# New order lists for a fused attention, expert and state-space layer

## The chip, the cores and the metric

The kernel runs on one core of a Trainium2 chip. The metric is the device time of one execution in microseconds (us), lower is better. Engines are named as in the profile: PE (TensorE), ACT (ScalarE), DVE (VectorE), POOL (GpSimd) and SP (SyncE, which here issues every transfer).

## The reference

For x of 16 batches x 512 tokens x 128 features, four residual blocks follow one another:

```
x = x + attn(layernorm(x))       # 16 heads of 8; elu(.)+1, rotary; (q_rot k_rot^T)/(q k^T), then v, then w_out
x = x + ffn(layernorm(x))        # 8 experts, top 2, plus one shared; 128 -> 512 -> 128, exact gelu
x = x + scan(layernorm(x))       # W_in, causal conv of 4, silu, 16 states of h = dA*h + dt*B*x, y = C*h, norm, gate, W_out
x = x + ffn(layernorm(x))        # the same expert block again
```

## The kernel before

One batch is a tile of 128 features x 512 tokens. The batches go through a software pipeline of passes, and in pass i several batches are at different blocks at once. A part is named by a letter:

- **P**: preparation of batch i+1 (`P.load` turns x in, `P.mean`, `P.var`, four `P.qk` projections, four `P.til`, two `P.rope`, then eight `P.cast` on ACT that alternate with eight `P.rest` on POOL: they split the rotated tiles into bf16 parts). `P.pk` 0 to 3 on SP write those parts to DRAM, six transfers each. `P.keep` on POOL copies x aside, after the attention of the batch before is closed. `P.ahead` 0 and 1 and `A.load` 0 and 1 on SP bring the repacked heads back, groups k = 0 to 3. `load_heads` for k = 0 waits until all 24 writes have landed.
- **A**: attention of batch i, 64 units in 16 steps. In a unit `A.den` (PE, L708) makes the denominator scores in one of two banks, `A.ln` (ACT) takes their logarithm, `A.num` (PE, L713) makes the numerator scores in the only bank NUM, and `A.mul` (DVE, L1110) multiplies. `A.ex` (ACT) is the exponential of a step of four units, `A.av` (PE, L735) the product with v of a step. `A.oT`, then `A.close` on PE (L741) and DVE (L1115), end it; `A.v` is the v projection.
- **F**: first expert block (batch i-1), **M** and **N**: the scan (batch i-1 begins it as M, its last nine states follow in the next pass as N), **E**: the end of the scan, **G** and **H**: second expert block (begun as G, ended one pass later as H). In F, G and H `up` and `down` are the products of 36 chunks (L772 to L774, L783), `gelu` is on ACT, `part` on DVE, `add` on POOL; `w` on SP loads an expert's weights from a DRAM copy, `gate` its gate row.
- **W** (pass 0 only): `W.split` on DVE makes the high and low halves of an expert's first weight, `W.store` on SP writes them to the DRAM copy. The first `F.w` waits for all nine.
- **T** on ACT: a load of a table set (L1023), `T.gelu`, `T.log` or `T.silu`.

No planner runs at build time. The order of each engine's queue is written out in six dictionaries: `HEAD` (before pass 0), `FIRST` (pass 0), `SECOND` (pass 1), `MAIN` (passes 2 to 15; pass 2 without H, pass 15 without P), `LAST` (pass 16) and `END` (pass 17). `numbered` expands an entry such as `A.ln*4` into the next four numbers of that part; `passes` runs the lists. Every engine works strictly through its own list, and each entry first waits on its semaphores, so an entry whose data is late holds up all that stands behind it:

```
            run(head, -1)
            run(numbered(FIRST[name], 0), 0)
            run(numbered(SECOND[name], 0), 1)
            main = numbered(MAIN[name], KEPT)
```

The waits that matter at the opening of a pass are these: the first `A.den` waits for heads k = 0, `F.mean` on PE waits for the DVE's `A.close` (`s_x1_done`), `P.cast` n waits for `P.rest` n-1, `W.split` n (from 3 on) for the landing of `W.store` n-3, and `P.ahead` 1 for the last `A.num` of the batch.

Of the kernel before, what the change touches and what calls it, by code (L numbers as in the profile page):

```python
# [1383 lines left out]
```

## Time and profile before

| | us |
|---|---|
| median of 3 runs (lowest to highest) | 3860.93 (3859.01 to 3870.79) |
| the profiled execution, its own time | 3871.34 |
| its span, first to last instruction | 3869.4 |
| PE busy | 3456.1 (89%) |
| ACT busy | 3236.8 (84%) |
| DVE busy | 2746.1 (71%) |
| POOL busy | 1277.1 (33%) |
| table loads on ACT | 554, 710.8 us |

Busy shares are means over passes that differ much: the passes at either end hold only some of the parts. PE busy includes modelled matmul ends. A stage is therefore read by its own window, its own waits and its own timeline.

### The profile page before, as it was taken

What the parts mean: (1) busy time and instruction counts of PE and PEld (TensorE: products, weight loads), DVE (VectorE), ACT (ScalarE), POOL (GpSimd) and SP (SyncE); (2) the same over time, 40 slices, a digit from 0 to 9 for tenths busy, and PEclk for the clock granted to TensorE, in tenths of its full rate; (3) what the DMA queues carried; (4) which work ended last, traced back from release to release, by engine and by line L of the source; (5) the groups of instructions that cost most, each with busy time, mean ns of one, the idle gap of its engine ahead of it and who ended that gap; (6) DMA issues with size and microseconds to landing.
All of it is one profiled execution on the core that took longest, in us unless ns stands there. A gap on an engine that the chain in (4) does not pass through costs nothing. (4 is left out here: it accounts for less than half of the span.)

```text
span 3869.4 us, 38405 instructions
## 1 busy us (share of the span) xinstructions
PE 3456.1 (89%) x11446; PEld 1442.6 (37%) x11446; DVE 2746.1 (71%) x3513; ACT 3236.8 (84%) x4060; POOL 1277.1 (33%) x758
## 2 busy tenths in 40 slices
...
GB/s 147 46 136 61 117 123 184 143 148 160 121 174 131 176 138 178 152 122 195 116 185 123 179 148 140 168 122 175 142 169 133 185 145 134 179 99 160 122 127 101
DMA packets 214848, 552.02 MB, mean 143 GB/s; under 512 B 25105, under 2 KB 96626, under 8 KB 214642
## 3 DMA queue, kind: packets, MB, share of 16 engines
...
## 5 line engine op out<-in xcount | busy, mean ns | idle before, releaser
L783 PE MATMUL bank<-hF,wst 128*128 128x512 f32 x2304 | 1171.9, 625 | 25.3 <-DVE tmp L1180 20.8
L1110 DVE TENSOR_TENSOR rPool<-bank,rPool 128x512 f32<-128x512 f32 x1024 | 703.1, 687 | 559.7 <-PE bank L713 514.1
L885 ACT ACTIVATE hF<-bank,cols 128x512 f32<-128x512 f32 x1152 | 770.9, 686 | 253.9 <-PE bank L774 245.5
L1330 POOL TENSOR_TENSOR yM<-yM,ws 128x1024 f32<-128x1024 f32 x240 | 595.1, 2479 | 1026.1 <-DVE ws L1229 1023.7
L1023 ACT ACT_TABLE_LOAD x554 | 710.8, 1283 | 9.7
L885 ACT ACTIVATE rPool<-bank 128x512 f32<-128x512 f32 x1024 | 571.2, 596 | 162.4 <-PE bank L708 156.9
L772 PE MATMUL bank<-xnH,wst 128*128 128x512 f32 x1152 | 599.5, 520 | 68.5 <-DMA wst<-wscr 36.4
L1222 DVE TENSOR_TENSOR_SCAN ws<-dAs,ws 128x1024 f32<-128x1024 f32 x256 | 635.5, 2487 | 6.9 <-ACT dAs L885 5.5
L1315 POOL TENSOR_TENSOR acc<-acc,tmp 128x512 f32<-128x512 f32 x240 | 353.1, 1471 | 835.7 <-DVE tmp L1180 827.3
L783 PEld LDWEIGHTS bank<-hF,wst 128*128 128x128 f32 x2304 | 412.7, 193 | 434.4 <-issue 347.7
L713 PE MATMUL bank<-qpk,kpk 48*128 48x512 bf16 x1024 | 420.3, 410 | 122.6 <-DVE rPool L1110 122.0
L885 ACT ACTIVATE rPool<-rPool 128x2048 f32<-128x2048 f32 x256 | 489.8, 1913 | 3.6
L774 PE MATMUL bank<-xnH,wst 128*128 128x512 f32 x1152 | 460.5, 400 | 0.0
L708 PE MATMUL bank<-qpk,kpk 48*128 48x512 bf16 x1024 | 383.6, 415 | 85.4 <-issue 49.6
L773 PE MATMUL bank<-xnL,wst 128*128 128x512 f32 x1152 | 459.7, 399 | 0.0
L1218 DVE TENSOR_TENSOR ws<-bc,dtx 128x1024 f32<-128x1024 f32 x256 | 376.0, 1478 | 19.9 <-DMA bc<-bcscr 19.7
L772 PEld LDWEIGHTS bank<-xnH,wst 128*128 128x128 f32 x1152 | 220.0, 191 | 343.6 <-issue 192.5
L735 PE MATMUL bank<-rPool,vpad 128*32 128x512 f32 x2048 | 325.5, 677 | 2.0
L1180 DVE SCALAR_TENSOR_TENSOR tmp<-bank,cols,cB 128x512 f32<-128x512 f32 x256 | 190.4, 744 | 173.9 <-PE bank L783 162.9
L885 ACT ACTIVATE dAs<-dte,Acol 128x1024 f32<-128x1024 f32 x256 | 294.3, 1150 | 21.3 <-DVE ws L1222 18.3
L1229 DVE TENSOR_TENSOR ws<-bc,ws 128x1024 f32<-128x1024 f32 x240 | 308.0, 1289 | 2.6
L713 PEld LDWEIGHTS bank<-qpk,kpk 48*128 48x128 bf16 x1024 | 95.7, 93 | 550.5 <-DVE rPool L1110 389.3
...
## 6 DMA issues: line engine op xcount, KB each, us to landing
...
kpk<-kscr SPq DMA_DIRECT2D x128, 192.0 KB, 6.0
qpk<-qscr SPq DMA_DIRECT2D x128, 192.0 KB, 6.5
...
```

The lines of the kernel that those rows point to most:

```text
L708: pe.matmul(ps[n % 2][:, :], lhs, rhs, start=True, stop=True).then_inc(s_den, 1)
L713: pe.matmul(ps[NUM][:, :], lhs, rhs, start=True, stop=True).then_inc(s_num, 1)
L772: pe.matmul(bank, low, xnH[:, :], start=True, stop=False)
L773: pe.matmul(bank, high, xnL[:, :], start=False, stop=False)
L774: pe.matmul(bank, high, xnH[:, :], start=False, stop=True).then_inc(s_up, 1)
L783: pe.matmul(ps[FFN][:, :], w2, hF[:, (NCH * f + q) % HSLOTS, :], start=(c == 0), stop=(c == FC - 1)).then_inc(s_dn, 1)
L885: return nc.scalar.activation(out_, in_, fn, **kw)
L1023: act.preload_act_table_set({"log": LOG_EXP, "gelu": GELU_SET, "silu": SILU_SET}[name])
L1110: v.tensor_tensor(rP[:, slot, c, :], ps[NUM][:, :], rP[:, slot, c, :], ALU.mult).then_inc(s_mul, 1)
L1218: v.tensor_tensor(w, bc[:, s % 2, 0:1, :].broadcast_to(both), dtx[:, :, :], ALU.mult).then_inc(s_dbx, 1)
L1222: v.tensor_tensor_scan(w.rearrange("p h t -> p (h t)"), dAs[:, s % 2, :, :].rearrange("p h t -> p (h t)"), w.rearrange("p h t -> p (h t)") ...
L1330: g.tensor_tensor(yM[:, :, :], yM[:, :, :], ws[:, s % 3, :, :], ALU.add).then_inc(s_ya, 1)
```

## The change

All order lists get a new text. Operations, buffers, semaphores and the functions stay as they are. For every engine and every pass the new list holds the same entries the same number of times, with two exceptions on ACT: `SECOND` has 22 table loads where it had 24, and in `LAST` one `T.gelu` has become a `T.log` (50 table loads as before). Only the order within a pass changes. The core of the diff:

```
@@ HEAD @@
     "ACT": """
-    P.load P.mean P.var P.qk*4 P.cast*8
+    P.load P.mean P.var P.qk*2 P.cast*2 P.qk P.cast*2 P.qk P.cast*4
...
     "POOL": """
-    P.keep P.rope P.rest*4 P.rope P.rest*4
+    P.rope P.rest*4 P.rope P.rest*3 P.keep P.rest
@@ FIRST @@
     "SP": """
-    P.in W.store*7 A.load*2 P.pk*4 P.ahead*2 W.store*2
+    P.in W.store*7 A.load*2 W.store P.pk*4 P.ahead*2 W.store
     "PE": """
...
-    A.num*2 A.den*2 A.num A.av A.num A.den*2 A.num A.den A.num*2 A.av A.num A.den*3 A.num A.den A.num*2 A.den A.av
-    A.num A.den A.num A.den A.num*2 A.av A.num*3 A.av A.close
+    A.num A.den*3 A.num A.av A.num A.den*2 A.num*2 A.av A.den*2 A.num*2 A.den*4 A.num*2 A.av A.num A.den*2 A.num*3
+    A.den A.av A.num A.den*2 A.num*2 A.den A.num*4 A.av A.den A.num A.den A.num A.av A.num A.den*2 A.num A.av
+    A.num*4 A.av A.close
     "ACT": """
...
-    A.ex P.qk A.ln*4 A.ex P.qk A.ln*4 A.ex P.cast A.ln*4 A.ex A.ln*4 A.ex A.ln*4 A.ex P.cast A.ln*4 A.ex P.cast
-    A.ln*4 A.ex A.ln*4 A.ex P.cast A.ln*4 A.ex A.ln*4 A.ex P.cast*3 A.oT P.cast
+    A.ex P.qk A.ln*4 A.ex A.ln*4 P.cast A.ex A.ln*4 A.ex A.ln P.qk A.ln*2 P.cast*2 A.ln A.ex A.ln*6 A.ex A.ln*2 A.ex
+    A.ln P.cast A.ln*3 P.cast A.ln*2 P.cast A.ln A.ex A.ln A.ex A.ln*4 P.cast*2 A.ex A.ln*4 A.ex A.oT
     "DVE": """
-    W.split*2 A.v W.split A.mul*3 P.mean A.mul W.split A.mul W.split A.mul*2 P.var A.mul W.split A.mul*4 W.split
-    A.mul*4 W.split A.mul*4 P.til A.mul P.til A.mul P.til A.mul*6 W.split A.mul*4 P.til A.mul*32 A.close
+    W.split*4 A.v W.split*2 A.mul*2 W.split A.mul W.split A.mul P.mean A.mul*3 P.var A.mul*6 P.til A.mul*4 P.til
+    A.mul*6 P.til A.mul*9 W.split A.mul P.til A.mul*31 A.close
     "POOL": """
-    P.rope*2 P.rest*7 P.keep P.rest
+    P.rope P.rest*2 P.rope P.rest*6 P.keep
@@ SECOND @@
     "SP": """
-    F.w P.in F.w*3 F.rows F.gate*2 F.w*2 F.gate*2 F.w*2 F.gate F.w F.gate*3 A.load M.rows M.bc*2 A.load P.pk M.bc*5
-    P.pk*3 P.ahead*2
+    P.in F.w*3 F.rows F.gate*2 F.w*3 F.gate*3 F.w*2 F.gate*2 F.w F.gate A.load M.rows M.bc*3 A.load P.pk M.bc*2 P.pk
+    M.bc P.pk M.bc P.pk P.ahead*2
     "PE": """
-    A.v A.den*2 F.mean A.den A.num A.den*2 F.var A.den*2 F.router F.up*2 A.num F.up*2 A.num F.up F.down*2 A.den
+    A.v A.den F.mean A.den*3 A.num F.var A.den F.router F.up*4 A.num F.up A.den*2 F.down*2 A.den A.num F.up A.den*2
...
-    A.av A.num A.den*4 A.num*6 A.av*2 A.close
+    A.den*2 A.num*2 A.av A.num A.den*2 A.num A.den*2 A.num*7 A.av A.num A.av A.num A.av A.close
     "ACT": """
...
-    A.ln*4 M.decay A.ex A.ln M.decay P.cast A.ln*3 A.ex A.ln*4 A.ex A.ln*4 P.cast A.ex A.oT P.cast*2
+    M.decay*2 P.cast A.ln*2 A.ex A.ln*2 A.ex A.ln*2 P.cast A.ln*2 A.ex M.decay A.oT
     "POOL": """
-    F.add*5 P.rope F.add*2 M.take P.rest*4 P.rope M.acc*3 M.keep M.acc P.rest*3 M.acc P.rest P.keep M.acc
+    F.add*4 P.rope P.rest F.add*3 M.take P.rest P.rope M.acc*2 P.rest*6 M.acc*2 M.keep P.keep M.acc*2
@@ MAIN @@
     "SP": """
...
-    F.gate*2 F.w F.gate F.w F.gate F.w F.gate P.pk G.w F.gate G.rows G.gate*2 G.w*2 M.rows G.w A.load P.pk M.bc*4
-    G.w G.gate M.bc G.w*2 P.pk G.gate M.bc*2 P.pk G.gate P.ahead G.gate G.w P.ahead
+    A.load F.w F.gate*3 F.w F.gate*2 F.w P.pk G.w*2 G.rows P.pk*2 G.gate*2 G.w M.rows M.bc A.load M.bc*2 G.w*2
+    M.bc*2 G.w G.gate*2 P.pk M.bc*2 G.w P.ahead*2 G.w G.gate*2
     "PE": """
-    A.v H.down*2 A.den*2 H.down A.den*2 H.down H.up*2 F.mean A.num A.den H.down*2 H.up*2 A.num H.up*4 F.var A.num
+    H.down*2 A.den H.down A.den H.down A.den*3 A.v A.num A.den H.down F.mean H.up H.down H.up A.den A.num A.den
...
     "DVE": """
-    A.v H.part F.mean A.mul N.dbx A.mul N.scan N.dbx N.hc A.mul*2 H.part N.scan F.var N.hc H.part F.router A.mul
+    H.part A.v A.mul F.mean A.mul N.dbx*2 N.scan N.hc H.part A.mul N.scan F.var N.hc A.mul H.part F.router A.mul
...
@@ LAST @@
     "ACT": """
...
-    T.log G.router T.gelu G.gelu*3 M.mean T.log M.var T.gelu G.gelu M.xp*3 T.silu M.silu M.xp M.silu T.gelu G.gelu
-    M.row G.gelu M.dt G.gelu*2 M.dt T.log M.sp M.decay*2 T.gelu G.gelu*2 T.log M.decay T.gelu G.gelu*3 T.log
+    T.log G.router T.gelu G.gelu*3 M.mean T.log M.var T.gelu G.gelu M.xp*3 T.silu M.silu M.xp M.silu M.row T.gelu
+    G.gelu M.dt G.gelu*2 M.dt G.gelu T.log M.sp M.decay*2 T.silu M.silu T.log M.decay T.gelu G.gelu*4 T.log
```

## Rows read from the trace of the kernel before

**Rows 1.** The page's groups: table loads (count, busy, mean ns, idle before).

```profile
L1023 ACT ACT_TABLE_LOAD x554 | 710.8, 1283 | 9.7
```

**Rows 2.** Stages (pass 0; 1; 2; 3-14; 15-17): length; PE, PEld, DVE, ACT, POOL; clock; DMA.

```profile
75.80:198.10 122.30, 96.60 (x282) 18.53 (x283) 56.00 (x85) 77.56 (x101) 15.89 (x13) 0.65 0.23 69
198.10:416.90 218.80, 165.91 (x505) 58.18 (x504) 105.24 (x142) 151.36 (x190) 38.76 (x29) 0.73 0.31 94
416.90:647.10 230.20, 199.08 (x649) 80.93 (x649) 161.91 (x209) 193.43 (x242) 73.90 (x44) 0.89 0.46 141
...
647.10:3299.30 2652.20, 2514.71 (x8569) 1055.59 (x8568) 2017.37 (x2581) 2407.47 (x3037) 929.16 (x564) 0.98 0.50 153
3299.30:3869.40 570.10, 461.10 (x1409) 221.24 (x1407) 388.42 (x433) 392.95 (x471) 201.24 (x88) 0.91 0.39 130
```

**Rows 3.** Who waited for whom, 196 to 240 us: total, times, longest.

```profile
DVE xnF L1128 <- PE bank L674: 15.2, 1, 15.2
...
PE bank L708 <- DMA kpk<-kscr: 12.9, 1, 12.9
```

**Rows 4.** Timeline of DVE at the end of pass 0: A.close.

```profile
198.35 0.75 DVE L1115 SCALAR_TENSOR_TENSOR xFin<-bank,cols,xA 128x512 f32<-128x512 f32 x1 [4.77 <-PE bank L741]
```

**Rows 5.** Timeline of POOL at the end of pass 0: start, duration.

```profile
199.29 0.61 POOL L1310 COPY xA<-xP 128x512 f32<-128x512 f32 x1 [6.15 <-DVE xFin L1115]
199.86 1.15 POOL L1305 TENSOR_TENSOR parts<-til,parts 128x512 bf16<-128x512 f32 x1
```

**Rows 6.** Timelines of SP's issues, then of PE, at the opening of pass 1.

```profile
206.51 0.31 SPq L584 DMA_DIRECT2D kpk<-kscr  x1
...
221.05 0.32 SPq L595 DMA_DIRECT2D wst<-wscr  x1
...
196.24 2.07 PE L741 MATMUL bank<-oT,wos 128*128 128x512 f32 x2 [0.69 <-ACT oT L885]
...
212.89 1.01 PE L708 MATMUL bank<-qpk,kpk 48*128 48x512 bf16 x2 [12.88 <-DMA kpk<-kscr]
...
225.51 0.79 PE L772 MATMUL bank<-xnH,wst 128*128 128x512 f32 x1 [1.73 <-DMA wst<-wscr]
```

**Rows 7.** Timelines of ACT, POOL, SP and PE at the opening of pass 2.

```profile
414.14 0.60 ACT L885 ACTIVATE oT<-bank 128x512 f32<-128x512 f32 x1 [8.19 <-PE bank L735]
...
416.58 0.63 ACT L885 ACTIVATE parts<-til 128x512 bf16<-128x512 f32 x1 [1.32 <-POOL til L1305]
...
433.89 1.09 ACT L885 ACTIVATE rPool<-bank 128x512 f32<-128x512 f32 x2 [14.09 <-PE bank L708]
...
418.75 2.14 POOL L1305 TENSOR_TENSOR parts<-til,parts 128x512 bf16<-128x512 f32 x1
...
426.40 0.32 SPq L584 DMA_DIRECT2D kpk<-kscr  x1
...
433.21 1.01 PE L708 MATMUL bank<-qpk,kpk 48*128 48x512 bf16 x2 [14.64 <-issue]
```

**Rows 8.** Timeline of PE in the second half of pass 0: A.num, A.num, A.av, A.num.

```profile
172.54 0.60 PE L713 MATMUL bank<-qpk,kpk 48*128 48x512 bf16 x1 [0.79 <-DVE rPool L1110]
...
173.92 0.60 PE L713 MATMUL bank<-qpk,kpk 48*128 48x512 bf16 x1 [0.79 <-DVE rPool L1110]
...
174.46 1.93 PE L735 MATMUL bank<-rPool,vpad 128*32 128x512 f32 x8
...
176.32 0.60 PE L713 MATMUL bank<-qpk,kpk 48*128 48x512 bf16 x1
```

**Rows 9.** Timelines of SP and PE where pass 10 opens.

```profile
2193.15 0.32 SPq L584 DMA_DIRECT2D kpk<-kscr  x1
...
2199.94 0.59 PE L708 MATMUL bank<-qpk,kpk 48*128 48x512 bf16 x2 [0.52 <-issue]
```

**Rows 10.** Busy time and clock around the opening of pass 2.

```profile
345.00:417.00 72.00, 45.19 (x125) 7.78 (x125) 53.17 (x51) 41.57 (x50) 14.86 (x9) 0.52 0.20 65
...
433.00:470.00 37.00, 28.53 (x67) 10.94 (x68) 27.36 (x47) 30.73 (x38) 6.71 (x3) 0.50 0.42 128
```

More of the change, by code:

```diff
@@ L121 @@
-    M.scan A.mul M.hc A.mul*4 M.hc A.mul*3 M.dbx A.mul*4 M.scan A.close M.hc
+    A.v F.mean F.var A.mul*2 F.router F.route A.mul*2 F.turn F.part P.mean A.mul*3 F.part A.mul*3 F.part P.var
+    A.mul*3 F.part*2 A.mul*3 P.til*2 F.part A.mul F.part*2 A.mul*2 F.part M.mean A.mul P.til A.mul M.var A.mul
+    M.conv A.mul M.conv*4 A.mul M.conv*2 A.mul M.conv A.mul*4 P.til A.mul*3 M.dt M.dbx A.mul M.dbx A.mul M.scan*2
+    M.hc*2 A.mul*3 M.dbx A.mul M.scan A.mul*2 M.hc A.mul*2 M.dbx A.mul*2 M.dbx A.mul*3 M.scan A.mul M.hc A.mul*2
@@ L148 @@
-    G.up*2 A.close
+    H.down*2 A.den H.down A.den H.down A.den*3 A.v A.num A.den H.down F.mean H.up H.down H.up A.den A.num A.den
+    H.up*6 H.down*2 A.num F.var H.up*2 H.down*4 F.up A.num A.den*2 F.router A.av A.num A.den H.down*3 A.num A.den
+    H.down F.up F.turn F.up*2 A.num H.close P.load A.den*2 A.num F.down*2 P.mean F.down*2 A.num A.den P.var A.den
+    A.num F.up A.den F.up A.num A.av A.num F.up*5 A.av P.qk F.up A.num F.down*4 A.num A.den*2 P.qk A.den A.num
+    F.down A.den F.down A.num P.qk A.num A.den*2 F.up A.num A.av A.den A.num F.up*3 F.down*2 A.num F.up*2 F.down
@@ L169 @@
-    A.mul M.scan M.hc A.mul*2 G.part M.dbx A.mul M.scan M.hc A.mul M.dbx A.mul G.part A.mul M.scan A.mul M.hc
-    A.mul*5 G.part A.mul*2 M.dbx*2 M.scan*2 M.hc*2 A.close
+    H.part A.v A.mul F.mean A.mul N.dbx*2 N.scan N.hc H.part A.mul N.scan F.var N.hc A.mul H.part F.router A.mul
+    F.route N.dbx H.part F.turn A.mul N.dbx A.mul N.scan*2 A.mul P.mean N.hc A.mul*2 N.hc A.mul*2 F.part N.dbx P.var
+    N.dbx N.scan*2 N.hc A.mul F.part A.mul N.hc A.mul*4 N.dbx*2 A.mul N.scan P.til*2 F.part A.mul N.hc A.mul*2
@@ L171 @@
+    N.scan A.mul F.part A.mul*2 N.dbx N.scan P.til N.hc*2 F.part A.mul*2 E.mean F.part P.til A.mul*3 E.var A.mul
+    E.gate F.part A.mul G.mean A.mul*2 F.part A.mul G.var G.router G.route F.part G.turn M.mean A.mul M.var M.conv*8
+    G.part A.mul*7 M.dt M.dbx A.mul M.dbx M.scan M.hc A.mul*2 G.part M.scan A.mul M.dbx A.mul M.hc M.scan M.hc
+    A.mul*2 G.part A.mul*2 M.dbx*2 A.mul M.scan M.hc A.mul*2 G.part A.mul M.scan A.mul*4 M.hc A.mul*2 G.part A.mul*2
+    M.dbx*2 M.scan*2 M.hc*2 A.close
 """,
@@ L172 @@
     "POOL": """
-    N.acc H.add N.acc H.add*3 N.acc*4 F.add P.rope N.acc*3 F.add*2 P.rope P.rest F.add P.rest*2 F.add P.rest F.add*2
-    M.take P.rest*2 M.keep G.add M.acc P.rest M.acc*2 P.rest M.acc G.add*3 P.keep M.acc*2
+    H.add N.acc*2 H.add*3 N.acc*2 F.add N.acc*2 P.rope F.add N.acc*3 F.add*2 P.rest*4 F.add P.rope F.add*2 M.take
+    P.rest*3 G.add M.acc P.rest M.acc G.add M.acc M.keep M.acc G.add*2 M.acc*2 P.keep
 """,
@@ L208 @@
-    M.scan M.dbx M.hc M.scan G.part M.dbx M.scan M.hc*2
+    F.mean H.part N.dbx*2 N.scan*2 N.hc H.part N.dbx N.hc H.part F.var N.scan N.dbx H.part F.router N.scan N.hc
+    F.route N.hc N.dbx F.turn F.part N.scan N.dbx N.hc N.scan F.part N.dbx N.scan N.hc F.part N.hc F.part N.dbx*2
+    N.scan*2 N.hc*2 F.part E.mean F.part E.var F.part E.gate G.mean G.var F.part G.router G.route F.part G.turn
+    M.mean M.var M.conv*8 G.part*2 M.dt M.dbx*2 M.scan*2 M.hc*2 M.dbx M.scan M.dbx M.hc M.scan M.dbx M.scan M.hc*2
```

147 lines of the change are left out of this document (66 added, 81 removed).

## The prediction

> **What bounds the kernel now.** I read the page first, then the busy time by stage, then, for the stages with most idle time, who waited for whom, and last the timelines at the openings of the passes. By stage [rows 2] the twelve full passes take 2652.2 us, 221.0 each, and ACT is busy 2407.5 us of them (91%). There ACT's queue sets the pace; what is left of its idle time is many short waits of 0.3 to 1.3 us for a product of PE, because PE is in turn held at `A.num` by DVE. Pass 0 is different: in its second half PE has no other work, and the single bank NUM makes every unit a round trip PE, DVE, PE. The products start 1.38 us apart, and 2.40 us where an `A.av` lies between them [rows 8]. Pass 1 takes 218.8 us with ACT busy for only 151.4, pass 2 takes 230.2 with 193.4, and passes 15 to 17 take 570.1 with 392.9 [rows 2]. The loose time is there.
>
> Two single waits stand out. At the opening of pass 1 PE sits 12.9 us at the first `A.den`, until the heads of batch 1 land [rows 3, 6]. `F.mean` stands behind it in PE's list, so DVE's `F.mean` waits 15.2 us too [rows 3]. At the opening of pass 2 PE sits 14.64 us at the same place and ACT 14.09 us [rows 7]. In a steady pass the same load costs 0.52 us [rows 9].
>
> Both go back along one chain: last `P.rest`, last `P.pk` (six issues and their landing), `P.ahead` 0, heads landed. In pass 0 the last `P.rest` starts at 199.86 us, straight after `P.keep`, which could not run before the attention was closed [rows 5]; it ends at 201.0, `P.ahead` goes out at 206.51, PE goes on at 212.89 [rows 6]. The chain is 11.9 us. In pass 1 the last `P.cast` stands behind `A.oT` in ACT's list, at 416.58; its `P.rest` ends at 420.9 and PE goes on at 433.21 [rows 7]: 12.3 us.
>
> **The change part by part.**
>
> *Opening of pass 1.* In the new `FIRST` the last two casts stand behind `A.ln` 59, two steps before the end, and `P.keep` behind the last `P.rest`. Of PE's list 12 `A.num` and three `A.av` come after the `A.den` of that unit and before the last product: 12 x 1.38 + 3 x 1.02 = 19.6 us, and some 3.5 us more to `A.close`, so about 23 us before `A.close`. The two casts (0.63 each) and rests (1.15 each) and their hand-overs take 4 to 5 us, the chain 11.9. Heads can land some 7 us before `A.close`, which stands at 196.24 now [rows 6]. The wait goes, with a margin. What is late next? `F.mean` then waits for `A.close` on DVE, 198.35 + 0.75 = 199.1 [rows 4]; PE starts it at 199.3 instead of right behind the `A.den` pair of 212.89, at 213.9: 14.6 us sooner. The second candidate is the first expert weight. It is issued at 221.05 [rows 6], after the last two stores have landed, and the first `F.up` follows at 225.51, 1.73 of which it waits for that weight [rows 6]; all else was ready at 223.8, 9.9 us behind `F.mean`. In the new list only store 8 stands behind `P.ahead` 1, which waits for the last `A.num`, 3.5 us before the 196.24 of `A.close`. Ahead 1, the store and its landing (half the bytes that took 11 us there) give about 203, and the weight lands 4.5 us after its issue, by 209; `F.up` would be wanted at 199.3 + 9.9 = 209.2. That is level, so I take 14 us and not 16.
>
> *Head and pass 0.* The new head puts two casts before the third `P.qk` and two before the fourth, so the second `P.rope` waits for its tile and no longer for POOL, and the first heads come about 1 us sooner. Against it, the new `FIRST` puts four `W.split` ahead of `A.v` and two more ahead of the first `A.mul`. From the fourth on a split waits for a store's landing, and DVE holds all behind it. `A.v` on PE is two entries earlier in exchange. I take the one as used up by the other, with 2 us either way. For the rest of pass 0 I sum the round trips of PE's two lists, each the larger of 1.38 us and the work between two products (0.43 us for a `den`, a little under the 0.54 from the product at 173.92 to the `av` at 174.46; 1.02 more where an `av` is [rows 8]): 124.7 us for the old order, 128.3 for the new, because the new one puts up to three `A.den` into gaps that hold an `A.av` already. At the upper clock the two sums are 87.6 and 88.2. Pass 0 has both clocks, 0.65 on average [rows 2]. I take +1.5 us, between +0.6 and +3.6.
>
> *Opening of pass 2.* The new `SECOND` has the last cast behind `A.ln` 61. Behind it stand 10 products and 3 `av`, 10 x 1.38 + 3 x 1.02 + 1.6 for a scan = 18.5 us, and about 4 us to `A.close`. Less 4 us for cast, rest and an `M.acc` in POOL's way, less the chain of 12.3, the heads land some 6 us before `A.close`. SP reaches the last `P.pk` in time, since the `M.bc` ahead of it needs only the fifth state's end, 12 units before the last. So the wait goes here too. ACT wins its 14.1 us. The F path wins less: PE's new opening has six `A.den` and `A.v` ahead of `F.mean`, which puts `F.mean` about 7 us behind the opening, where it is 18.3 now: 11 us. ACT is the busier engine of pass 2 (193.4 of 230.2), so the value is nearer to the first: 12.5 us.
>
> *The rest of pass 1.* Two table loads of 1.28 us fewer [rows 1] lie in the stretch after `M.xp`, where ACT is busy 41.6 of 72 us [rows 10] and waits for PE: nothing. The same sum of round trips from `M.dt` on (products, `av`, and scan entries on DVE) gives 69.5 against 68.0 us at the lower clock and 59.6 against 62.2 at the upper. I take 0, with 3 us either way.
>
> *Passes 3 to 14.* Entry counts are the same, so ACT's busy time is the same; only its waits can change. I compared the lists where waits arise: for each run of three or more `gelu` the PE work between its second and last `up`, less what the `gelu` take. The excess adds up to 32.6 us in the old `MAIN` and 32.8 in the new; adjacent `A.num` pairs are 4 and 3; casts, norms and scans lie within three units of where they were. At the edges, `P.pk` 3 now stands ahead of `M.bc` 5 and 6, so `P.ahead` 0 can go a few us sooner than the 2193.15 of now, but it shares the queue with a weight. It is worth at most the 0.52 us [rows 9]. The opening puts `A.v` behind five `A.den`, about 0.5 us later for `F.mean`. I take 0, with 3 us a pass either way as the bound: the spread of the short waits that one pass has.
>
> *Passes 15 to 17.* DVE sets pass 16. In `LAST` the `M.row` copy moves ahead of a table load and a `gelu`, 2 us sooner, and a `gelu` moves into the chain behind it: -1 us. The last pass keeps its pattern. Bound 5 us either way.
>
> **A rule beside the trace.** At the openings the granted clock is half: 0.52 in the 72 us before the pause and 0.50 in the 37 us after it [rows 10]. So PE was at 1.2 GHz of its two levels already before it paused. The Trainium skill, TensorE: Matmul & The Clock Gate, "Part 1: The HAM clock gate", says that an idle TensorE is put on half clock and that sustained work brings it back. By it, an opening without a pause could be at full clock sooner. In the 37 us ACT is busy 30.7 [rows 10], so a faster PE could win at most the other 6 us there; I put nothing of it into the sum.
>
> **Sum.** Against the profiled execution of 3871.3 us: -14 + 1.5 - 12.5 + 0 + 0 - 1 = -26, so 3845. That execution is 10 us above the median of the three runs; against the median of 3860.9 the forecast is 3835 us.
>
> **The rivals.**
>
> 1. *The steady passes lose it.* The new `MAIN` opens with DVE's `H.part` ahead of `A.v`; it waits for a gate row that SP issues only behind `P.ahead` 1, that is, behind the last `A.num`, with three transfers ahead of it. And one `G.up` stands behind `A.close`. If this and shifted runs of `up` cost more than 26 / 14 = 1.9 us a pass, the gain is gone; at 4 us a pass the time is 3861 - 26 + 56 = 3891. For it: all entries wait in order, and the row is due within 5 us of the opening. Against it: equal sums. Chance 0.11.
> 2. *The pauses only move.* The heads are on time, but the first weight (store 8 behind `P.ahead` 1), or casts that are held by POOL, are late instead, and half the gain goes: about 3848. For it: the weight is level with the need. Against it: it can cost 1 to 5 us only at pass 1. Chance 0.14.
> 3. *The steady passes gain as well.* If 2 us of short waits go in each of 14 passes: 3835 - 28 = 3807. For it: ACT idles some 18 us in each pass. Against: the sums show no difference. Chance 0.18.
> 4. *The forecast*, both pauses gone and all else level: 3835, own range 3822 to 3846. Chance 0.57.
>
> **How the numbers follow.** The forecast case and the third lie wholly below 3849, and of the second a little over half; 0.3% (12 us, about what a measurement of this kernel can tell from no change) begins there. That gives faster 0.80, same 0.11, slower 0.09. The range from 3800 to 3865 leaves out most of the first rival and the far end of the third, less than 2 in 10.
>
> **What the profile after would show.** Right: the first `A.den` of passes 1 and 2 with under 2 us of idle time before it; the last `P.rest` of pass 0 ahead of the last multiplies; pass 1 some 13 us and pass 2 some 12 us shorter; the twelve steady passes within 10 us of 2652. Wrong: a wait of `F.up` for the weight load over 3 us in pass 1; steady passes more than 2 us from 221.0 each; pass 0 more than 4 us longer. The forecast fails most likely by the steady passes, since twelve of them multiply a small miss.

## The result: slower by 1.6%, and the profile after

The changed kernel takes 3920.4 us (median of 4 runs, 3918.8 to 3926.2), the kernel before 3860.0 (4 runs, 3853.7 to 3870.8). The ratio is 1.0158, with a 95% interval of 1.0139 to 1.0177. The forecast was 3835. The profiled execution took 3926.2 us and its span is 3924.2, which is 54.8 us more than the span before. The medians differ by 60.4, so the two profiles show most of the loss.

The same five stages as in [rows 2], in the changed kernel (length; PE, PEld, DVE, ACT, POOL; clock; DMA):

```profile
75.60:204.90 129.30, 97.31 (x283) 19.04 (x282) 54.99 (x83) 76.20 (x101) 16.75 (x14) 0.65 0.31 87
204.90:402.50 197.60, 159.35 (x503) 55.11 (x503) 98.67 (x142) 150.09 (x189) 38.92 (x28) 0.82 0.32 100
402.50:619.30 216.80, 190.50 (x644) 78.62 (x643) 157.42 (x210) 191.30 (x240) 76.86 (x43) 0.93 0.44 139
619.30:3331.80 2712.50, 2508.71 (x8571) 1062.62 (x8569) 1958.24 (x2581) 2412.84 (x3038) 982.14 (x564) 0.98 0.47 150
3331.80:3924.20 592.40, 468.59 (x1412) 226.63 (x1411) 365.37 (x433) 393.38 (x471) 188.52 (x88) 0.89 0.37 125
```

Pass 3 begins at 619.3 us, where it began at 647.1 [rows 2] (646.8 by ACT's first entry, from which passes are counted below): the openings give their 27 us. Then twelve full passes take 2712.5 us instead of 2652.2 [rows 2], 226.0 each and no longer 221.0, which costs 60. Passes 15 to 17 take 592.4 instead of 570.1, another 22. PE's busy time in the twelve passes is even a little lower (2508.7 against 2514.7), and ACT's is 5 us higher: what has grown is waiting.

**The openings.** PE in the changed kernel, end of pass 0 to the first `up` of pass 1, and the same at the next pass:

```profile
202.80 2.07 PE L741 MATMUL bank<-oT,wos 128*128 128x512 f32 x2 [0.69 <-ACT oT L885]
...
206.52 0.60 PE L708 MATMUL bank<-qpk,kpk 48*128 48x512 bf16 x1
207.46 1.10 PE L674 MATMUL bank<-xFin,onesD 128*128 128x512 f32 x2 [0.34 <-DVE vpad L1100]
...
214.60 0.77 PE L772 MATMUL bank<-xnH,wst 128*128 128x512 f32 x1
...
401.32 1.13 PE L741 MATMUL bank<-oT,wos 128*128 128x512 f32 x2 [0.69 <-ACT oT L885]
402.38 0.60 PE L708 MATMUL bank<-qpk,kpk 48*128 48x512 bf16 x2
...
424.62 0.77 PE L772 MATMUL bank<-xnH,wst 128*128 128x512 f32 x1 [9.50 <-issue]
```

SP and POOL in the same stretch: `P.ahead` 0 in pass 0, the last store, the first weight, and the last `P.rest`:

```profile
188.52 0.31 SPq L584 DMA_DIRECT2D kpk<-kscr  x1
...
201.26 0.42 SPq L631 DMA_DIRECT2D wscr<-wst  x1
...
206.96 1.31 SPq L595 DMA_DIRECT2D wst<-wscr  x3
...
181.85 1.16 POOL L1305 TENSOR_TENSOR parts<-til,parts 128x512 bf16<-128x512 f32 x1 [0.80 <-ACT parts L885]
```

The waits of 12.88 and 14.64 us for heads [rows 6, 7] are gone. `P.ahead` 0 is issued 14 us before `A.close`, where it came 10 us behind it. Counted from `A.close`, the first `up` of pass 1 comes 11.8 us later (202.80 to 214.60) instead of 29.3 [rows 6].

Pass 2 has a new pause, though. It is the 9.50 us in front of the last line of the first view. Pass 2 already runs `MAIN`, whose new order puts F.up 0 ahead of `F.router` on PE, so PE stands there until DVE has F.up 0's input ready. DVE has scan entries to do first: from 412 to 425 us it is busy for 12.90 of 13 us and PE for 3.08, and the last part of the input (`xnL`, L1120) is done at 424.51. The first `up` of pass 2 still comes 15.9 us sooner behind `A.close` than before.

**The steady passes.** Who waited for whom in passes 3 to 14 (total, times, longest). The kernel before, rows not shown yet:

```profile
PEld bank L772 <- DMA wst<-wscr: 25.8, 21, 2.6
PE bank L772 <- DMA wst<-wscr: 18.3, 20, 2.4
```

The changed kernel:

```profile
PEld bank L772 <- DMA wst<-wscr: 88.3, 60, 3.3
PE bank L772 <- DMA wst<-wscr: 50.4, 45, 2.4
DVE tmp L1180 <- issue: 32.1, 11, 3.8
```

L772 is an `up`, `wst` an expert's weights. PE waits for a weight load 45 times instead of 20, and DVE's `part` has a wait that was not there. The pass boundary before pass 10 shows both. SP, then PE, then DVE of the changed kernel:

```profile
2173.55 3.75 SPq L571 DMA_DIRECT2D kscr<-parts  x6
2177.48 8.35 SPq L619 DMA_DIRECT2D bc<-bcscr  x2
2185.87 0.43 SPq L595 DMA_DIRECT2D wst<-wscr  x1
2186.57 0.32 SPq L584 DMA_DIRECT2D kpk<-kscr  x1
...
2191.39 0.42 SPq L595 DMA_DIRECT2D wst<-wscr  x1
2192.01 0.84 SPq L606 DMA_DIRECT2D cB<-gscr  x2
...
2222.73 0.32 SPq L595 DMA_DIRECT2D wst<-wscr  x1
...
2193.42 0.51 PE L772 MATMUL bank<-xnH,wst 128*128 128x512 f32 x1 [2.02 <-DMA wst<-wscr]
...
2224.45 0.50 PE L772 MATMUL bank<-xnH,wst 128*128 128x512 f32 x1 [1.74 <-DMA wst<-wscr]
...
2203.83 0.75 DVE L1180 SCALAR_TENSOR_TENSOR tmp<-bank,cols,cB 128x512 f32<-128x512 f32 x1 [3.81 <-issue]
```

and SP of the kernel before, one pass boundary as well:

```profile
2168.51 9.00 SPq L595 DMA_DIRECT2D wst<-wscr  x2
2177.63 3.84 SPq L571 DMA_DIRECT2D kscr<-parts  x6
...
2182.28 3.13 SPq L619 DMA_DIRECT2D bc<-bcscr  x2
2185.53 3.99 SPq L571 DMA_DIRECT2D kscr<-parts  x6
```

Read SP from the top. `M.bc` 5 and 6 (`bc<-bcscr` x2) take 8.35 us to issue. SP waits 7.4 us of them for DVE's `M.hc` (L1229), which frees the buffer that the next coefficients go into. The load G.w 6 stands behind them, goes out at 2185.87, and PE waits 2.02 us for it at 2193.42. Before, G.w 6 (the second of the x2) was issued ahead of the `bc` pair. There are three slots for weights, so a load reuses the slot of the expert three places earlier. Averaged over passes 3 to 14, in us from ACT's first entry of the pass, with the list entries counted off against the trace:

| load | its slot is free, before / after | issued, before / after | its first `up` waits, before / after |
|---|---|---|---|
| F.w 0 | 21.2 / 22.7 | 21.2 / 23.9 | 0 / 1.44 (F.up 0) |
| F.w 3 | 48.5 / 50.0 | 48.6 / 68.0 | 0 / 0.94 (F.up 12) |
| F.w 4 | 58.6 / 66.7 | 68.6 / 70.4 | 1.05 / 0 (F.up 16) |
| G.w 6 | 201.1 / 207.1 | 201.1 / 218.5 | 0 / 1.38 (G.up 24) |

F.w 0 goes out within 1.2 us of its slot being free in both, but 2.7 us later in the pass, and F.up 0 has moved ahead of `F.router` on PE. F.w 3 stands behind `F.gate` 2 and 3, and the buffer for the latter is taken until 67.7. DVE's wait is for the gate rows that SP now issues last in the pass (`G.gate` 5 at 224.7 instead of 213.7, for the first `H.part` of the next pass); it costs PE 0.87 us at H.down 24. Together the four places are 1.44 + 0.94 + 1.38 + 0.87 = 4.6 us of PE's idle time in a pass, against 1.05 before. Two smaller places change sides: PE waited 0.42 us a pass for H.w 8 before and no longer does, and F.w 8, without a wait before, now costs 0.30.

The late loads also take longer from issue to landing: F.w 0 6.4 us instead of 4.2, F.w 3 5.9 instead of 4.5, G.w 6 6.9 instead of 4.8, and the gate row G.gate 5 10.9 instead of 4.1. For each of the three loads the added 1.5 to 2.1 us are more than PE's wait. So a wait is the sum of a later issue and a longer way; which neighbours in the queue lengthen the way was not looked for.

### The profile page after: what moved, and what is told of

It is laid out like the page before. It is cut to its first block, busy times and chain, and to the rows that moved or that the text cites. A ratio compares the mean times of both kernels' runs of the same rounds, so it can differ in the third digit from the quotient of the medians.

```text
span 3924.2 us, 38403 instructions
## 1 busy us (share of the span) xinstructions
PE 3443.9 (88%) x11446; PEld 1450.3 (37%) x11446; DVE 2653.8 (68%) x3513; ACT 3237.7 (83%) x4058; POOL 1321.8 (34%) x758
## 4 chain that ended last, share of the span: by engine, by line
PE 53%; DVE 16%; DMA 11%; ACT 9%; issue 8%; POOL 1%; SPq 1%; POOLq 0%; ACTq 0%; DVEq 0%
PE bank L783 16%; DMA wst<-wscr 7%; PE bank L772 6%; PE bank L735 5%; PE bank L713 5%; PE bank L774 4%; PE bank L773 4%; PE bank L674 4%; DVE rPool L1110 4%; DVE ws L1222 3%; ACT hF L885 3%; PE bank L708 2%; DVE tmp L1180 2%; DMA cB<-gscr 2%; ACT L1023 2%
## 5 line engine op out<-in xcount | busy, mean ns | idle before, releaser
L783 PE MATMUL bank<-hF,wst 128*128 128x512 f32 x2304 | 1185.6, 626 | 40.8 <-DVE tmp L1180 30.7
L1330 POOL TENSOR_TENSOR yM<-yM,ws 128x1024 f32<-128x1024 f32 x240 | 663.7, 2766 | 728.5 <-DVE ws L1229 721.7
L772 PE MATMUL bank<-xnH,wst 128*128 128x512 f32 x1152 | 616.1, 535 | 119.9 <-DMA wst<-wscr 74.0
L1222 DVE TENSOR_TENSOR_SCAN ws<-dAs,ws 128x1024 f32<-128x1024 f32 x256 | 598.4, 2351 | 4.1 <-DVE ws L1218 0.5
L713 PE MATMUL bank<-qpk,kpk 48*128 48x512 bf16 x1024 | 418.5, 409 | 124.9 <-DVE rPool L1110 121.3
L1315 POOL TENSOR_TENSOR acc<-acc,tmp 128x512 f32<-128x512 f32 x240 | 342.9, 1429 | 516.9 <-DVE tmp L1180 510.0
L774 PE MATMUL bank<-xnH,wst 128*128 128x512 f32 x1152 | 462.4, 401 | 0.0
L708 PE MATMUL bank<-qpk,kpk 48*128 48x512 bf16 x1024 | 369.4, 405 | 65.6 <-ACT rPool L885 36.0
L772 PEld LDWEIGHTS bank<-xnH,wst 128*128 128x128 f32 x1152 | 221.0, 192 | 400.3 <-issue 143.9
L1218 DVE TENSOR_TENSOR ws<-bc,dtx 128x1024 f32<-128x1024 f32 x256 | 319.2, 1264 | 23.6 <-DMA bc<-bcscr 23.0
L1229 DVE TENSOR_TENSOR ws<-bc,ws 128x1024 f32<-128x1024 f32 x240 | 324.9, 1365 | 1.6
L1305 POOL TENSOR_TENSOR til<-til,parts 128x512 f32<-128x512 f32 x64 | 76.8, 1200 | 734.2 <-ACT parts L885 734.2
```

The source lines that it names most:

```text
L708: pe.matmul(ps[n % 2][:, :], lhs, rhs, start=True, stop=True).then_inc(s_den, 1)
L713: pe.matmul(ps[NUM][:, :], lhs, rhs, start=True, stop=True).then_inc(s_num, 1)
L772: pe.matmul(bank, low, xnH[:, :], start=True, stop=False)
L774: pe.matmul(bank, high, xnH[:, :], start=False, stop=True).then_inc(s_up, 1)
L783: pe.matmul(ps[FFN][:, :], w2, hF[:, (NCH * f + q) % HSLOTS, :], start=(c == 0), stop=(c == FC - 1)).then_inc(s_dn, 1)
L1222: v.tensor_tensor_scan(w.rearrange("p h t -> p (h t)"), dAs[:, s % 2, :, :].rearrange("p h t -> p (h t)"), w.rearrange("p h t -> p (h t)") ...
```

## The experiments

The theory, called W, is that the steady passes lose because SP issues weight loads late. Against it stood O, that the new orders of the other engines cost the time themselves; later rivals are named where they come up. "A pass" is the mean of passes 3 to 14, 221.0 us before and 226.0 changed. Ratios are to the kernel before.

**1. The openings alone.** The kernel before with `HEAD`, `FIRST` and `SECOND` of the changed one.

```diff
@@ before: HEAD, FIRST, SECOND, every engine, as changed; FIRST's SP for one @@
-    P.in W.store*7 A.load*2 P.pk*4 P.ahead*2 W.store*2
+    P.in W.store*7 A.load*2 W.store P.pk*4 P.ahead*2 W.store
```

> The kernel before with HEAD, FIRST and SECOND of the change, and its own MAIN, LAST and END. If the passes are independent blocks: pass 3 starts some 27 us sooner, as after the change (646.8 to 619.3 us in the two traces), and the rest keeps its length: 3833 us (3826 to 3840), ratio 0.993. Rival: the early start is lost again in the steady passes, because their old order needs the old late start: within 5 us of 3860.

Measured: 3827.8 us, ratio 0.9908 (0.9892 to 0.9925). Pass 3 begins at 611.7, a pass is 220.2. With nothing else touched the openings are worth 34 us (the kernel before stood at 3861.6 beside it), more than the 26 of the forecast and inside the range expected.

**2. All but MAIN.** The changed kernel with `MAIN` as before.

```diff
@@ after: MAIN, every engine, as before; its SP begins @@
-    N.bc*2 H.gate H.w H.gate F.w P.in F.w N.bc*2 H.out F.rows N.bc F.w F.gate N.bc F.gate*2 F.w N.bc*2 F.w N.bc F.w
+    N.bc*2 H.w P.in H.gate F.w H.gate N.bc*2 F.rows F.w H.out N.bc F.gate F.w*2 N.bc*3 F.gate F.w*2 A.load N.bc
```

> The changed kernel with MAIN of before on all five engines. If the loss lies in MAIN's order (passes 3 to 15 took about 70 us more in the trace of the change): 3920 - 70 = 3850 us (3842 to 3858), steady passes back to about 220 us. Rival: MAIN is slower because of what comes before it, by phase or clock, whatever its list: it stays at 3900 or more.

Measured: 3843.3 us, 0.9949 (0.9931 to 0.9968); a pass is 220.8 and PE's waits for weights in passes 3 to 14 are back at 17.4 us in 18 times. The loss of the steady passes is in `MAIN`.

**3 and 4. SP's list alone.** In 3 the changed kernel has SP's `MAIN` as before; in 4 the kernel before has SP's `MAIN` as changed.

```diff
@@ 3, after: MAIN, SP; ends @@
-    M.bc*2 G.w G.gate*2 P.pk M.bc*2 G.w P.ahead*2 G.w G.gate*2
+    G.w G.gate M.bc G.w*2 P.pk G.gate M.bc*2 P.pk G.gate P.ahead G.gate G.w P.ahead
@@ 4, before: MAIN, SP; ends @@
-    G.w G.gate M.bc G.w*2 P.pk G.gate M.bc*2 P.pk G.gate P.ahead G.gate G.w P.ahead
+    M.bc*2 G.w G.gate*2 P.pk M.bc*2 G.w P.ahead*2 G.w G.gate*2
```

> The changed kernel with only SP's MAIN list of before. Theory W: the steady pass lost its 5 us because SP issues the expert weights and gate rows later (behind M.bc and P.ahead waits): at least 3 us a pass come back in 13 passes, 3870 us or less, and the waits of the weight matmul for wst go from 74 us of PE idle time back to under 45. Rival O: the order of PE, ACT and DVE at the opening of the pass costs it: under 1.5 us a pass comes back, 3900 or more.

> The kernel before with only SP's MAIN list of the change. Theory W: 3 to 5 us a pass slower, 3900 to 3930 us, PE waiting for wst at chunk 24 of the second expert block. Rival O: within 15 us of 3860.

Measured: 4083.0 us (1.0563, 1.0545 to 1.058; a pass 237.9) and 3981.7 us (1.0304, 1.0285 to 1.0324; a pass 229.6). Both are slower than either kernel. An SP list fits only the lists it was written with, so exchanging it whole tells no cause apart. W missed in both; O missed in 4, and in 3 its "3900 or more" holds in the letter alone, since it didn't expect the kernel to become slower. The pair does show how much SP's order weighs: some 163 and 120 us with every other engine's list untouched. From here on single entries are moved.

**5. G.w 6 and the gate row, in time.** One line of SP's `MAIN` in the changed kernel. G.w 6 moves ahead of `M.bc` 5 and 6; G.gate 5 and G.w 7 move ahead of `P.ahead` 1.

```diff
-    M.bc*2 G.w G.gate*2 P.pk M.bc*2 G.w P.ahead*2 G.w G.gate*2
+    M.bc*2 G.w G.gate*2 P.pk G.w M.bc*2 P.ahead G.gate G.w P.ahead G.gate
```

> The changed kernel, with the end of SP's MAIN list alone altered: the seventh G.w ahead of M.bc 5 and 6, the first late G.gate and the last G.w ahead of P.ahead 1. Theory W (late weights and gate rows at the seam of two passes): the 1.4 us that PE waits at G.up 24 and some 0.9 us at H.down 24 go in each of 13 passes, 2 us a pass, 3895 us (3885 to 3903). Rival O (order of PE, ACT and DVE): within 8 us of 3920.

Measured: 3885.0 us, 1.0049 (1.0032 to 1.0066), 35 us below the changed kernel; a pass is 222.7. G.up 24 and H.down 24 no longer wait, F.up 0 (1.56) and F.up 12 (0.86) do as before. The first product with G.w 7, H.up 28, had no wait in the changed kernel either.

**6. F.up 0 behind `F.router` again.** PE's `MAIN` in the changed kernel.

```diff
-    H.up*6 H.down*2 A.num F.var H.up*2 H.down*4 F.up A.num A.den*2 F.router A.av A.num A.den H.down*3 A.num A.den
-    H.down F.up F.turn F.up*2 A.num H.close P.load A.den*2 A.num F.down*2 P.mean F.down*2 A.num A.den P.var A.den
+    H.up*6 H.down*2 A.num F.var H.up*2 H.down*4 A.num A.den*2 F.router A.av A.num A.den H.down*3 A.num A.den
+    H.down F.up*2 F.turn F.up*2 A.num H.close P.load A.den*2 A.num F.down*2 P.mean F.down*2 A.num A.den P.var A.den
```

> The changed kernel, with F.up 0 in PE's MAIN list moved from ahead of F.router to just ahead of F.turn, next to F.up 1. Theory W (the slot is freed by H.down 27 and its reload of about 6 us is not over when F.up 0 comes, 1.4 us of PE idle time): 1 to 1.4 us a pass come back, 3903 us (3898 to 3910). Rival O: no gain, 3915 to 3925, or slower because the first gelu of F come later.

Measured: 3899.4 us, 1.0085 (1.006 to 1.011), 21 us below the changed kernel; a pass is 223.6, and F.up 0's wait is gone. W had expected 1 to 1.4 us a pass; it is 2.4. In pass 2 the pause of 9.50 us is gone too: the two longest there are 3.7 and 3.5.

**7 and 8. Lighter weights in both kernels.** Every load of expert weights outside the first block moves a quarter of the partitions, so the products in it are of mixed weights.

```diff
-                    sp.dma_start(wst[:, slot, :, :].bitcast(F32), wscr[NE if e == 0 else e - 1]).then_inc(s_w[slot], 16)
+                    n_rows = P if f == 0 else P // 4
+                    sp.dma_start(wst[0:n_rows, slot, :, :].bitcast(F32), wscr[NE if e == 0 else e - 1][0:n_rows]).then_inc(s_w[slot], 16)
```

> The changed kernel with every expert load but those of the first expert block cut to a quarter of the partitions (the other rows keep an earlier expert's weights, so the experts' products are of mixed weights). Theory W: the weights land some 3 us sooner, the waits for wst go, and at least 3 of the 5 us a pass come back: 3880 us or less, while the same cut in the kernel before gives under 15 us. Rival O: both kernels gain alike, and the distance of about 60 us stays.

> The kernel before with the same cut (experts' products of mixed weights). Theory W: 3845 to 3860 us, since its weights were mostly in time. Rival O: as much gain as in the changed kernel.

Measured: the changed kernel goes to 3827.0 us (0.99, 0.9884 to 0.9917), 93 us lower; the kernel before to 3843.5 (0.9938, 0.9921 to 0.9954), 23 below the 3866.8 that kernel took beside it. A pass is 218.7 and 219.0. W had allowed the kernel before less than 15 us of gain. With lighter loads the two `MAIN`s are equal, and the changed kernel wins by its openings. So the 60 us are transfers that land too late for the entry that needs them; the computing engines' new orders cost nothing beside that. That it is the weights alone does not follow: with less on the queue the gate rows come sooner too, and DVE's waits for them fall from 32.1 to 11.7 us in passes 3 to 14.

**9. All three places mended.** Experiments 5 and 6 together, and F.w 3 ahead of `F.gate` 2 and 3.

```diff
@@ after, with the lines of 5 and 6; MAIN, SP @@
-    N.bc*2 H.gate H.w H.gate F.w P.in F.w N.bc*2 H.out F.rows N.bc F.w F.gate N.bc F.gate*2 F.w N.bc*2 F.w N.bc F.w
+    N.bc*2 H.gate H.w H.gate F.w P.in F.w N.bc*2 H.out F.rows N.bc F.w F.gate N.bc F.w F.gate*2 N.bc*2 F.w N.bc F.w
```

> The changed kernel with three moves in MAIN: SyncE's new tail (its run alone gave 3885.0, 35 us off), F.up 0 beside F.up 1 (alone 3899.4, 21 us off), and F.w 3 issued ahead of F.gate 2 and 3 instead of behind them. Theory W (the steady passes lose because SyncE issues a few expert loads late, and nothing else is wrong with the new orders): the three places are independent, F.up 12's wait of 0.94 us a pass goes as well, passes 3 to 14 come to 220 to 221 us (226.0 in the changed kernel), and the time is 3850 to 3865 us. Rival R (the loads share the queue, so that what is issued earlier only makes the next load late): at most the larger of the single gains is kept, passes 3 to 14 stay at 222.5 us or more and the time at 3880 us or more.

Measured: 3823.1 us, 0.9899 (0.9882 to 0.9915). That is 97 us below the changed kernel, by three loads (F.w 3, G.w 6, G.w 7) and a gate row issued earlier and one product moved later. W was right in kind, and the gain is 27 us larger than the most that it gave: it had counted each wait at little more than its own length. R, by which an earlier load only delays the next, is refuted here. A pass is 218.8. The steady waits of this kernel, and its SP at the boundary before pass 10:

```profile
PEld bank L772 <- DMA wst<-wscr: 15.2, 22, 1.2
PE bank L772 <- DMA wst<-wscr: 5.3, 9, 0.9
```

```profile
2123.49 3.75 SPq L571 DMA_DIRECT2D kscr<-parts  x6
2127.28 0.59 SPq L595 DMA_DIRECT2D wst<-wscr  x1
2128.05 7.72 SPq L619 DMA_DIRECT2D bc<-bcscr  x2
```

The load now goes out right behind the stores, and the `bc` pair waits behind it, as it did anyway. Of the 7.2 us a pass from 226.0 to 218.8, the moves of 5 and 6 gave 3.3 and 2.4 when each ran alone, more than the idle time of their places (2.25 and 1.44). F.w 3 was never moved alone. If the other two keep their worth it gives the remaining 1.5, for a wait of 0.94.

**10. The same mend in the kernel before.** Experiment 1 with F.w 4 issued ahead of the third `N.bc` and `F.gate` 2.

```diff
-    N.bc*2 H.w P.in H.gate F.w H.gate N.bc*2 F.rows F.w H.out N.bc F.gate F.w*2 N.bc*3 F.gate F.w*2 A.load N.bc
+    N.bc*2 H.w P.in H.gate F.w H.gate N.bc*2 F.rows F.w H.out N.bc F.gate F.w*2 N.bc*2 F.w N.bc F.gate F.w A.load N.bc
```

> The kernel before with the new HEAD, FIRST and SECOND (3827.8 us), and in MAIN's list for SyncE the load F.w 4 moved ahead of the third N.bc and F.gate 2; it stands behind them in the kernel before, where its slot is free 10 us before it is issued and F.up 16 then waits 1.0 us a pass. Theory W: F.up 16's wait goes, and with 13 such passes the time falls by 8 to 13 us, to 3815 to 3820 us, passes 3 to 14 at 219.2 to 219.6 us. Rival R: the load's place in the queue is taken from N.bc or F.gate 2, VectorE waits for a row instead, and the time stays within 4 us of 3828 or is above it.

Measured: 3816.7 us, 0.988 (0.9858 to 0.9902), the lowest median of all, 11 us under experiment 1. F.w 4 goes out at 60.0 instead of 68.6, F.up 16's wait (1.05 in the kernel before) is gone, a pass is 219.3 instead of 220.2. Here a wait of about 1 us gives back 0.9, no more than its length. Its steady waits (17.9 us in experiment 1):

```profile
PEld bank L772 <- DMA wst<-wscr: 12.1, 12, 1.9
PE bank L772 <- DMA wst<-wscr: 5.3, 6, 1.5
```

**11. LAST as before.** The changed kernel with `LAST` of the kernel before.

```diff
@@ after: LAST, every engine, as before; ACT's for one @@
-    T.log G.router T.gelu G.gelu*3 M.mean T.log M.var T.gelu G.gelu M.xp*3 T.silu M.silu M.xp M.silu M.row T.gelu
+    T.log G.router T.gelu G.gelu*3 M.mean T.log M.var T.gelu G.gelu M.xp*3 T.silu M.silu M.xp M.silu T.gelu G.gelu
```

> The changed kernel with LAST's lists as before on all engines. LAST's pass (16) took 261.9 us before and 270.8 after. Theory L (the loss of pass 16 is in its own lists): pass 16 falls back to 261 to 263 us and the time to about 3911 us (3907 to 3915), passes 3 to 14 stay at 226. Rival M (pass 16 is longer because MAIN's last pass hands it a later state): pass 16 stays above 268 us and the time is within 4 us of 3920.

Measured: 3924.8 us (3915.6 to 3936.7), 1.017 (1.0148 to 1.0192): no lower than the changed kernel, nearly as rival M had it. But in the profile pass 16 takes 261.9 us, as before and as L had it, where the changed kernel's takes 270.8. The profiled span is 3913.5, shorter by 10.7, and this execution was the fastest of the four. So `LAST`'s lists do lengthen pass 16 by 9 us, and the timed runs don't give them back.

**12. One step of the change alone.** The kernel before, with G.w 6 behind `M.bc` 5 and 6.

```diff
-    G.w G.gate M.bc G.w*2 P.pk G.gate M.bc*2 P.pk G.gate P.ahead G.gate G.w P.ahead
+    G.w G.gate M.bc G.w P.pk G.gate M.bc*2 G.w P.pk G.gate P.ahead G.gate G.w P.ahead
```

> The kernel before with one single step of MAIN's SyncE list moved as the changed kernel has it: the load G.w 6 stands behind M.bc 5 and 6 instead of ahead of them. Theory W: the load is then issued only when ScalarE has the coefficients of those M.bc, some 10 us later, G.up 24 waits 1 to 2 us in each of 13 passes, and the kernel is slower by 15 to 30 us, 3875 to 3895 us. Rival S (the load still has slack in the kernel before, since G.up 24 stands there 18 us after the slot is freed): G.up 24 doesn't wait, and the time is within 5 us of the kernel before.

Measured: 3884.5 us, 1.005 (1.0031 to 1.0069); a pass is 222.7. The price came out in W's range, the place did not. (The wait ahead of the load is for DVE's `M.hc`, as said above, and not for ScalarE.) G.w 6 is issued 10 us later, but G.up 24 has that slack and never waits. PE waits one step further on. SP and PE before pass 10, then the steady waits (before: 1.7 us, once):

```profile
2189.74 9.62 SPq L619 DMA_DIRECT2D bc<-bcscr  x2
2199.40 0.43 SPq L595 DMA_DIRECT2D wst<-wscr  x1
2199.95 4.31 SPq L571 DMA_DIRECT2D kscr<-parts  x6
...
2208.21 0.32 SPq L584 DMA_DIRECT2D kpk<-kscr  x1
...
2214.84 0.59 PE L708 MATMUL bank<-qpk,kpk 48*128 48x512 bf16 x2 [1.45 <-DMA kpk<-kscr]
```

```profile
PEld bank L708 <- DMA kpk<-kscr: 11.8, 5, 3.0
PE bank L708 <- DMA kpk<-kscr: 7.8, 5, 2.2
```

So the same step costs time in both kernels, but by another wait in each. The load is now issued right ahead of the six transfers of `P.pk`, and the heads go out 8.3 us behind the start of these, against 7.6 in the kernel before (2185.53 to 2193.15 [rows 9]). That the load and the stores share the DMA engines there is argued from the order, not shown.

**13. The three moves and the old LAST.** Experiment 9 with the `LAST` of experiment 11, to tell the 9 us where no weights are late.

```diff
@@ three moves, and LAST, every engine, as before @@
-    T.log G.router T.gelu G.gelu*3 M.mean T.log M.var T.gelu G.gelu M.xp*3 T.silu M.silu M.xp M.silu M.row T.gelu
+    T.log G.router T.gelu G.gelu*3 M.mean T.log M.var T.gelu G.gelu M.xp*3 T.silu M.silu M.xp M.silu T.gelu G.gelu
```

> The changed kernel with the three moves in MAIN and with LAST's lists as before. In the profile of the changed kernel with only LAST as before, pass 16 took 261.9 us (270.8 with the new LAST), but the timed runs of that kernel lay at 3924.8 us, no lower than those of the changed kernel. Theory L (pass 16's 9 us are real and belong to LAST's lists; the steady passes, late with their weights, varied by more than that from run to run): with steady passes that wait for no weights, the time falls by 6 to 10 us from 3823.1, to 3813 to 3817 us. Rival M (what LAST gains is given back in pass 15, or is lost in MAIN's last pass): pass 15 or 17 is longer by as much, and the time is 3820 us or more.

Measured: 3819.1 us, 0.9886 (0.9858 to 0.9914), 4 us below experiment 9, between the two theories. In the profile pass 16 is 262.2 instead of 271.0, and pass 15 is 223.3 instead of 220.4. Part of the 9 us is where the pass is counted from. The new `LAST` begins with a table load on ACT, which waits for nothing, and the old one with `N.decay`, so pass 16 starts sooner in the new one and pass 15 is shorter by it. Passes 15 to 17 together take 575.2 us here and 580.8 in experiment 9, 585.6 in experiment 11 and 592.6 in the changed kernel. So the old `LAST` is worth 6 to 7 us in the profiles, less than the openings vary from run to run; in the timed runs it is not clear of noise. Experiments 9, 10 and 13 cannot be told apart by their intervals; each beats both kernels by 1.0% or more.

## Why the prediction was wrong

Most of its steps held, and one did not. It is the step that was multiplied by twelve. In us, from the two profiles:

| stretch | forecast | measured | how |
|---|---|---|---|
| to `A.close` of pass 0 | +1.5 | +6.6 | 196.24 [rows 6] to 202.80 |
| `A.close` to first `up`, pass 1 | -14 | -17.5 | 29.3 [rows 6] to 11.8 |
| rest of pass 1 | 0 | -2.6 | to `A.close` of pass 1, 414.79 to 401.32 |
| opening of pass 2 | -12.5 | -15.9 | first `up` at 453.99, 39.2 behind `A.close`; now 23.3 |
| rest of pass 2 | 0 | +1.9 | to the start of pass 3 |
| passes 3 to 14 | 0 | +60 | 2652.2 [rows 2] to 2712.5 |
| passes 15 to 17 | -1 | +22 | 570.1 [rows 2] to 592.4 |

The two rows of the kernel before on which the opening of pass 2 rests here (PE: `A.close`, first `up`):

```profile
414.79 2.08 PE L741 MATMUL bank<-oT,wos 128*128 128x512 f32 x2 [0.72 <-ACT oT L885]
...
453.99 0.80 PE L772 MATMUL bank<-xnH,wst 128*128 128x512 f32 x1
```

**The openings: right.** Both pauses went by the mechanism named, the last `P.rest` of pass 0 at 181.85 and `P.ahead` 0 at 188.52. Forecast for the five stretches was -25, measured -27.5. That it is so close is partly luck. Pass 0 lost more than was allowed for, 6.6 us, beyond its upper bound of 3.6, which was worked out from PE's list alone, and three of the other stretches made up for it by 2.6 to 3.5 us each. The same lists reach `A.close` of pass 0 at 198.0 in experiment 1, at 202.8 in the changed kernel and at 205.4 in experiment 10, and the old ones between 193.2 and 196.5 in four profiles (before, 4, 8, 12). Pass 3 begins between 611.7 (1) and 622.7 us (7) in most profiles with the new openings, at 625.5 in 6 and 631.5 in 3, and between 644.8 and 649.2 with the old ones. What makes the new ones vary by 7 us at `A.close` was not looked for. The first weight, called level with the need, went out at 206.96 and not at 203, and nothing waited for it. Two table loads fewer in pass 1 brought nothing that can be seen.

**The clock beside it.** The 27 us after PE goes on in pass 1, in the kernel before and then in the changed one:

```profile
213.00:240.00 27.00, 23.80 (x71) 10.38 (x69) 10.06 (x35) 18.04 (x24) 0.00 (x0) 0.67 0.49 156
```

```profile
207.00:234.00 27.00, 23.43 (x79) 10.37 (x78) 11.42 (x37) 23.35 (x30) 0.00 (x0) 0.93 0.39 131
```

The granted clock is 0.93 of full where it was 0.67, and more is done in the same 27 us. Between `A.close` and the first `up` the `ones` products (L674, two at a time) take 1.10 us where they took 2.07. That is part of the 3.5 us by which this opening beat the forecast. Experiment 1 has the same opening, also without a pause, and PE was granted 0.50 up to 216 us, 18 us behind `A.close` (198.01); its first `up` comes 14.6 us behind `A.close` and not 11.8. So without the pause the upper level comes sooner (in the kernel before the clock was still 0.50 up to 230 us, 34 us behind `A.close`), but how much sooner differs between the runs. By the rule named in the prediction (the Trainium skill, TensorE: Matmul & The Clock Gate, "Part 1: The HAM clock gate"), an idle TensorE goes to half clock and sustained work brings it back; pass 1 agrees in direction. At pass 2 the changed kernel shows less of it:

```profile
425.00:440.00 15.00, 12.68 (x47) 6.30 (x46) 10.44 (x32) 11.68 (x15) 2.35 (x1) 0.63 0.11 38
440.00:470.00 30.00, 28.93 (x98) 11.25 (x100) 24.43 (x25) 27.58 (x36) 11.70 (x5) 1.00 0.44 144
```

Full clock comes at about 440 us, 38 us behind the first `A.den` of 402.38, and no sooner than before, where the 37 us behind 433 were still at 0.50 [rows 10]. Between 402 and 412 us the clock was granted at 0.67 and then it fell back to 0.50 from 412 to 425 us, where PE was busy 3.08 of 13 us, with the pause of 9.50 us in it. Experiments 1 and 10, with the old `MAIN` and no such pause, had 0.83 and 0.84 in the 10 us behind `A.close` and 0.50 in the next 20, with PE busy 6.5 to 8.2 us of each 10.

**The failed step.** It is "*Passes 3 to 14.* Entry counts are the same, so ACT's busy time is the same; only its waits can change", with 0 taken and 3 us a pass as the bound. It measured +5.0 a pass. The working under it compared the lists of PE and ACT with each other, and DVE's, and never laid SP's list beside them, except for the gate row of the first rival. For a load three times matter: when the last `down` of the expert three places earlier frees the slot, when SP reaches the entry, and when the first `up` wants it, with 5.5 us (median, before) from issue to landing between the last two. Three such chains lost their slack in the new `MAIN`, and one regained it (F.w 4). Experiment 2 puts the loss in `MAIN`, 7 and 8 put it on the transfers, and 5, 6 and 9 on these entries. The one edge that was looked at, `P.pk` 3 ahead of `M.bc` 5 and 6, is the line on which G.w 6 stands. It was read for `P.ahead`, with the remark that "it shares the queue with a weight", and the weight was not followed. In place of the 0 the runs show 1.44 us of waiting at F.up 0, 0.94 at F.up 12, 1.38 at G.up 24 and 0.87 at H.down 24 in each pass, less the 1.05 that F.up 16 no longer waits: 3.6 us of the 5.0. The rest fits what such waits cost beyond their own length in 5 and 6; PE's whole idle time in these passes grew from 11.5 to 17.0 us each.

The Trainium skill says in DMA: Bandwidth & Descriptors, "Issuing engines are not separate DMA queues", that transfers issued by several engines run on the same DMA engines, so that issuing on several engines saves only the time that it takes to issue. No run here issues from a second engine. The loads lost time at SP without its being busy: of the 8.35 us with G.w 6 behind, it waited 7.4. Whether a second issuing engine would take that away is open.

**The rivals.** The first was the case: steady passes that lose more than 1.9 us each. It named the right wait of DVE (32.1 us in 11 waits, 3.81 at pass 10), but that is one of four places and the smallest on PE, 0.87 of 4.6 us. "Equal sums", which spoke against it, was true and beside the point: experiment 9 shows that the new sums are as good as the old ones (218.8 and 219.3 a pass with punctual loads). The third rival, a gain of 2 us a pass, is what the same lists, but for the moved entries, do in experiment 9 (218.8 against 221.0). The second came in part, by a way that it didn't name: at pass 1 nothing took the place of the pause, at pass 2 PE's wait of 14.64 us made room for one of 9.50 in front of the first `up`. It did not cost half the gain. Two of the prediction's numbers here are off: ACT's idle time is 20.4 us a pass by [rows 2] and not some 18, and "faster" adds up to a little over 0.82 and not 0.80.

**Passes 15 to 17.** Forecast -1 with a bound of 5, measured +22. Pass 15 still runs `MAIN` and lost 10.2 us; with the three moves it takes 220.4, so this is the same cause. Pass 16 lost 8.9 and has them back with the old `LAST` in both profiles (11, 13); of this 6 to 7 us are left over passes 15 to 17, which entry it is was not looked for, and the time did not clearly follow. Pass 17 took 87.0 us before and 90.2 after, but with `LAST` and `END` as before it took 90.7 in experiment 10, so these 3 us are the spread of one profile.
